# A decoder layer on one core: the first split spread by TensorE, scores on all 128 columns, three groups of heads in one half of a bank

## What is computed

```python
x = _layernorm(x + attn(x))            # latent attention, causal, 256 keys
x = _layernorm(x + xattn(x, ctx_1024)) # 512 context keys + 256 own keys, own ones causal
x = _layernorm(x + ffn(x))             # 64 small MLPs of 16 hidden units each
```

## Time and profile before

| | us |
|---|---|
| median of 3 runs | 291.99 |
| lowest, highest | 291.78, 295.43 |
| the profiled execution | 293.45 |
| its span, first to last instruction | 291.7 |

### The profile page before, as it was taken

The page is one execution under the profiler, slowest core; times in us unless marked ns, Lnnn a source line. Parts: engine busy times, 40 slices in busy tenths (PEclk is TensorE's granted clock), DMA queues, the critical chain, the costliest instruction groups (busy, mean ns, idle before and its releaser), DMA issues.

```text
span 291.7 us, 13772 instructions
## 1 busy us (share of the span) xinstructions
PE 241.0 (83%) x5973; PEld 144.2 (49%) x5973; DVE 194.3 (67%) x429; ACT 159.8 (55%) x367; POOL 99.8 (34%) x250
## 2 busy tenths in 40 slices
PE   8920478689845699999999499999999999999882
PEld 5710336456533446756555156454654465544651
DVE  0830395785232578797999277999889997852652
ACT  1400024455523257676788255988688858879330
POOL 8650074635321142334372101522225212531131
PEclk9985595999977799999999669999999999999998
DMA  4169995101897017353639600000000000000000
GB/s 138 64 202 299 243 205 141 24 8 42 248 186 174 12 57 169 107 117 102 124 106 224 115 3 3 5 5 5 5 3 5 5 5 5 3 5 21 21 18 18
DMA packets 22716, 23.66 MB, mean 81 GB/s; under 512 B 1472, under 2 KB 20224, under 8 KB 22528
## 3 DMA queue, kind: packets, MB, share of 16 engines
q1 hardware_dynamic: 22224, 22.55, 31.7%
q10 hardware_dynamic: 432, 0.23, 0.3%
HBM read 12.62 MB, written 9.96 MB: 77 GB/s over the span
## 4 chain that ended last, share of the span: by engine, by line
PE 42%; DVE 19%; DMA 14%; SPq 9%; issue 7%; ACT 3%; POOL 3%; ACTq 2%; POOLq 0%; DVEq 0%
PE psum L1011 13%; PE psum L1086 10%; DVE pm L869 9%; DMA qk<-shift_rows 6%; DMA qk<-scr_qk 5%; DVE pm L871 4%; PE psum L1106 4%; PE psum L1018 3%; PE psum L958 3%; ACTq L599 2%; ACT probs L774 2%; DMA scr_m<-spl 2%; SPq L635 1%; PE psum L1173 1%; SPq L634 1%
## 5 line engine op out<-in xcount | busy, mean ns | idle before, releaser
L774 ACT ACTIVATE probs<-psum 128x512 f32<-128x512 f32 (+1 forms) x256 | 120.6, 554 | 41.6 <-PE psum L1011 20.9
L1011 PE MATMUL psum<-qk 51*32 51x128 bf16 (+3 forms) x2048 | 63.2, 266 | 31.7 <-DMA qk<-scr_qk 20.9
L871 DVE TENSOR_REDUCE pm<-psum 128x3 f32<-128x384 f32 x128 | 63.5, 550 | 36.6 <-PE psum L1018 36.5
L869 DVE TENSOR_REDUCE pm<-psum 128x1 f32<-128x512 f32 x128 | 79.1, 681 | 7.0 <-PE psum L1011 7.0
L1086 PE MATMUL psum<-probs,v 128*9 128x256 f32 (+1 forms) x1024 | 66.1, 368 | 3.5 <-issue 2.8
L1011 PEld LDWEIGHTS psum<-qk 48*32 48x32 bf16 (+1 forms) x2048 | 35.2, 96 | 56.1 <-DMA qk<-scr_qk 21.5
L1011 PE MATMUL psum<-qk,km 51*32 51x256 bf16 x1024 | 37.9, 278 | 2.8 <-DMA qk<-shift_rows 2.5
L724 POOL TENSOR_SCALAR_AFFINE_SELECT probs<-probs 128x512 f32<-128x512 f32 x32 | 20.3, 640 | 57.0 <-ACT probs L774 56.7
L1086 PEld LDWEIGHTS psum<-probs,v 128*9 128x9 f32 x1024 | 23.2, 91 | 26.0 <-issue 13.8
L1011 PE MATMUL psum<-km,qk 48*32 48x512 bf16 x512 | 35.6, 394 | 0.2
L1018 PE MATMUL psum<-neg,unit_b 64*32 64x256 bf16 x512 | 31.5, 305 | 0.0
(11 more groups left out here) (98 smaller groups left out, 263.7 us busy)
## 6 DMA issues: line engine op xcount, KB each, us to landing
qk<-scr_qk SPq DMA_DIRECT2D x16, 384.0 KB, 6.4
scr_qk<-spl SPq DMA_DIRECT2D x8, 384.0 KB, 5.1
scr_qk<-spl SPq DMA_DIRECT2D x24, 128.0 KB, 5.1
km<-scr_m SPq DMA_DIRECT2D x8, 384.0 KB, 6.8
scr_m<-spl SPq DMA_DIRECT2D x4, 384.0 KB, 3.1
ctxT_sb<-ctxT SPq DMA_DIRECT2D x1, 1024.0 KB, 5.7
scr_m<-spl SPq DMA_DIRECT2D x4, 256.0 KB, 3.5
wb_sb<-wb SPq DMA_DIRECT2D x1, 642.0 KB, 4.5
```

The source lines that it names most:

```text
L774: nc.scalar.activation(probs[:, ring % PRING, r, 0:cols], bank_of(s)[:, 0:cols], ACT.Exp, scale=SCALE).then_inc(exp_done, 1)
L869: nc.vector.tensor_reduce(pm[:, place, 1 + 4 * qt:2 + 4 * qt], m, axis=AX.X, op=ALU.max).then_inc(reduced, 1)
L871: nc.vector.tensor_reduce(pm[:, place, 2:5], own_blocks(m), axis=AX.X, op=ALU.max).then_inc(reduced, 1)
L1011: last = nc.tensor.matmul(o[STRIP * c:STRIP * (c + 1)], lhs[:, STRIP * c:STRIP * (c + 1)], rhs, start=start, stop=stop, skip_group_check=True)
```

## The change

- **First split (unit 0).** No put and take. TensorE lays its parts on their rows: for each of 8 pairs of heads ("rep") six bf16 matmuls against 0/1 matrices `spread`, which GpSimd builds at the start in the place of the context keys of batch 3; ScalarE or VectorE copies the result to `qk`, adding the constant rows by a bias. The scores of a step of unit 0 wait for the two reps of its group.
- **Scores.** `in_tiles` is gone: one matmul on 128 columns takes the place of four on 32. The mask is two matmuls, the second only over half of the block.
- **Heads.** The values lie in zeroed buffers such that the pv of groups 0, 1 and 2 accumulate in one half of bank 7 (up to 27 output rows to a head) and group 3 in the other. ScalarE drains 128 x 512 once to a unit; norm takes 4 matmuls. There are 3 buffers of values for units 4 to 7, blanked by GpSimd after steps 1, 3 and 5; the rows under the context keys come after steps 2, 4, 6 and 8.
- **Start.** 14 warm-up matmuls; the identity and unit matrices are cast by ScalarE; VectorE writes the constant rows for units 1 to 3; the context is loaded right after the weights.
- **Engines.** The low parts of the splits of units 1 to 3 go from GpSimd to VectorE. The last step of a layer norm goes from VectorE to ScalarE, with `-mean * rstd` made by GpSimd (two instructions more).
- **Order.** New costs and `LATE`; `SPL` = 5; a feed-forward's last product waits for the last `wo`.

```diff
-SPL = 3
+SPL = 5
+V2BUFS = 3
...
-BLANK_AFTER = (2, 4, 6)
+VALUES_AFTER = (1, 3, 5)
+BLANK_AFTER = (2, 4, 6, 8)
...
-LATE = [(("qk", 0), 0), (("qk", 1), 0), (("v1", 0), 0), (("qk", 2), 0), (("v1", 1), 0),
-        (("m", 0), 2), (("vm", 0), 4), (("qk", 3), 6), (("m", 1), 8), (("vm", 1), 10), (("m", 2), 16), (("vm", 2), 17),
-        (("m", 3), 20), (("vm", 3), 21)]
+LATE = [(("qk", 0), 0), (("qk", 1), 0), (("qk", 2), 1), (("v1", 0), 0), (("qk", 3), 3), (("v1", 1), 1), (("m", 0), 5),
+        (("vm", 0), 11), (("m", 1), 6), (("vm", 1), 13), (("m", 2), 12), (("vm", 2), 15), (("m", 3), 22),
+        (("vm", 3), 25)]
...
+def replicated(s):
     return s == ("qk", 0)
...
+    return s[0] == "qk" and s[1] < B
...
+        spread = km[:, B - 1, 0:3, :].rearrange("p n (i c) -> p (n i) c", c=P).rearrange("p (i a n) c -> p i a n c", i=2, a=2)
+        v1 = sb("v1", [P, B * QT, VCOLS])
+        v2 = sb("v2", [P, V2BUFS, KT2, VCOLS])
...
+            pool.wait_ge(wa_in, 16)
+            hot = wa_sb[:, WA["hot"]:WA["hot"] + STRIP].rearrange("p (i r d) -> p i r d", i=2, r=2)
+            for a, order in enumerate(MEETING):
+                for slot, part in enumerate(order):
+                    cols = spread[:, :, a, part, :].rearrange("p i (r c) -> p i r c", r=2)
+                    nc.gpsimd.tensor_copy(cols[:, :, :, slot * HS:(slot + 1) * HS], hot).then_inc(spread_ready, 1)
...
-                    if n in BLANK_AFTER:
-                        ones_under_memory(1 + BLANK_AFTER.index(n))
+                    if n in VALUES_AFTER:
+                        blank_values(VALUES_AFTER.index(n))
+                    elif n in BLANK_AFTER:
+                        ones_under_memory(BLANK_AFTER.index(n))
...
+            nc.scalar.activation(ident_b[:, :], ident, ACT.Copy).then_inc(ident_ready, 1)
+            for r in range(2):
+                nc.scalar.activation(half(unit_b, r, HALF)[:, HALF:P], half(ident, r, HALF)[:, HALF * r:HALF * (r + 1)],
+                                     ACT.Copy).then_inc(ident_ready, 1)
             fold_out(4, w1[:, 1, :])
-            fold_out(5, w1[:, 2, :])
...
-                    nc.scalar.activation(headsT[:, t % (2 * NG), :], heads[:, 0:T], ACT.Copy).then_inc(drained, 1)
+                    nc.scalar.activation(headsT[:, t // NG % 2].rearrange("p n t -> p (n t)"), heads, ACT.Copy).then_inc(drained, 1)
...
+                elif what == "apply":
+                    kind_, b = s[1], s[2]
+                    act.wait_ge(rstd_ready, ln_no[s[1:]] + 1)
+                    for i in range(QT):
+                        last = nc.scalar.activation(x1[:, b, i, :], res[:, i, :], ACT.Identity, bias=offset[:, i:i + 1],
+                                                    scale=rstd[:, i:i + 1])
...
-            ones_under(nc.vector, qk[:, 0, :, 1, :]).then_inc(qk_ones[0], 1)
+            for u in range(1, B):
+                ones_under(nc.vector, qk[:, u, :, 1, :]).then_inc(qk_ones, 1)
...
+                    elif what == "rep":
+                        dve.wait_ge(bias_ready, 1)
+                        nc.vector.tensor_copy(qk[:, 0, s[1], 0, :], m[:, 0:T])
+                        nc.vector.tensor_scalar_add(qk[:, 0, s[1], 1, :], m[:, T:], ones_bias[:, 0:1]).then_inc(dve_misc_done, 1)
...
-                    keep_warm(2, bank(n)[:, half_bank * T:(half_bank + 1) * T])
+                    keep_warm(1, bank(n)[:, half_bank * T:(half_bank + 1) * T])
...
+                    elif replicated(("qk", u)):
+                        for a in range(2):
+                            wait_misc(("rep", 2 * group(t) + a))
...
-            def in_tiles(o, lhs, rhs, start, stop):
-                for c in range(HG):
-                    last = nc.tensor.matmul(o[STRIP * c:STRIP * (c + 1)], lhs[:, STRIP * c:STRIP * (c + 1)], rhs, start=start,
-                                            stop=stop, skip_group_check=True)
-                return last
-            def mask(o, r, rows):
-                for c in range(HG):
-                    last = nc.tensor.matmul(o[STRIP * c:STRIP * (c + 1)], half(unit_b, r, HALF), half(rows, r, HALF)[:, c, :, :],
-                                            start=False, stop=True, skip_group_check=True)
+            def mask(o, r, what):
+                rows = half(neg if what == "S" else negT, r, HALF)
+                for n in range(2):
+                    units = half(unit_b, r, HALF)[:, HALF * (1 - n):HALF * (1 - n) + P]
+                    if (what == "S") == (n == 0):
+                        block, part = o, rows
+                    else:
+                        block, part = (o[:, :, HALF:], rows[:, 0:HALF]) if what == "S" else (o[:, :, 0:HALF], rows[:, HALF:])
+                    last = nc.tensor.matmul(block, units, part.unsqueeze(1).to_broadcast([HALF, 2, part.shape[-1]]), start=False,
+                                            stop=(n == 1), skip_group_check=True)
                 return last
...
-                in_tiles(m[:, 0:P], queries[:, 0:P], keys[:, 0:P], True, False)
-                in_tiles(m[:, P:P + T], queries[:, P:T], keys, False, False)
-                return mask(own_blocks(m)[:, 0:3:2, :], r, neg)
+                    return nc.tensor.matmul(m, queries[:, qt * P:(qt + 1) * P], half(km[:, u % B, p, :], r, DATA), start=True,
+                                            stop=True)
+                nc.tensor.matmul(m[:, 0:P], queries[:, 0:P], keys[:, 0:P], start=True, stop=False, skip_group_check=True)
+                nc.tensor.matmul(m[:, P:P + T], queries[:, P:T], keys, start=False, stop=False, skip_group_check=True)
+                return mask(own_blocks(m)[:, 0:3:2, :], r, "S")
...
-                    if k == 0 and t:
-                        pe.wait_ge(drained, t)
+                    if k == 0 and g == 0 and t:
+                        pe.wait_ge(drained, t // NG)
...
+                        at = VJ * j + VG * g
+                        end, at = at + HS + 1, at - (HS + 1) * (g if g < NG - 1 else 0)
+                        if k == 0 and g == 0:
+                            end = at + VG
+                        o = heads[STRIP * j:STRIP * j + end - at, (T if g == NG - 1 else 0):][:, q0:T]
...
-                        last = nc.tensor.matmul(heads[STRIP * j:STRIP * j + HS + 1, q0:T], v, weights, start=(k == 0),
-                                                stop=(k == len(key_tiles(t)) - 1))
+                        last = nc.tensor.matmul(o, v[:, at:end], weights, start=(k == 0 and g in (0, NG - 1)),
+                                                stop=(k == len(key_tiles(t)) - 1 and g >= NG - 2), skip_group_check=True)
...
                         for qt in range(QT):
-                            for g in range(NG):
-                                at, cols = ORDER.index((u, g)) % (2 * NG), HG * (HS + 1)
-                                n = qt * NG + g
-                                last = nc.tensor.matmul(m[:, n * cols:(n + 1) * cols], headsT[:, at, qt * P:(qt + 1) * P],
-                                                        used_rows, start=True, stop=True)
+                            for n, cols in ((0, (NG - 1) * HG * (HS + 1)), (1, HG * (HS + 1))):
+                                o = m[:, qt * NH * (HS + 1) + n * (NG - 1) * HG * (HS + 1):][:, 0:cols]
+                                last = nc.tensor.matmul(o, headsT[:, at % 2, n, qt * P:(qt + 1) * P], used_rows[n], start=True,
+                                                        stop=True)
...
+                        parts = spl[:, split_no[("qk", 0)] % SPL, :, :]
+                        for a in range(2):
+                            for n in range(PARTS):
+                                last = nc.tensor.matmul(m[:, a * T:(a + 1) * T], strip(spread[:, i, a, n, :], j, STRIP),
+                                                        strip(parts[:, 5 - 2 * n if a else 2 * n, :], j, STRIP),
+                                                        start=(a == 0 and n == 0), stop=(n == PARTS - 1), skip_group_check=True)
```

296 lines of the change are left out of this document (177 added, 119 removed).

## The result

| | before | after |
|---|---|---|
| median us | 291.88 (4 runs) | 278.77 (4 runs) |
| lowest, highest | 288.89, 295.43 | 275.87, 281.61 |
| the profiled execution, its span | 293.45, 291.7 | 280.01, 278.3 |

The ratio is 0.955, with a 95% interval from 0.940 to 0.970: faster by 4.5%, some 13 us. Some executions of every kernel here run a few per cent longer at a lower clock; the medians include them and the ratios don't, so that the two can differ.

The account below looks back on a forecast made before the run. Waits were taken to bound units 0 to 3 and VectorE's maxima units 4 to 7. Start 14 + units 0 to 3 56 + units 4 to 7 139.5 + mask 1 + tail 36 = 246.5, less 0.3: 246 us, range 231 to 270.

Parts of the forecast that it names:

- 26 + 30 = 56: Units 0 to 3: from first score to unit 4's start, a chain of 64 us unchanged, shortened to 56.
- 139.5: Units 4 to 7: 151.5 us less 7 for the applies and 5 for half of the hole.
- 1 for the mask: TensorE: the wide mask adds 5.6 us of columns over the run, 1 us of it on the path.
- Forecast 14: Start: the first score comes at 14 us, not 33.3, or 16.9 us earlier with slow casts.
- no gap of over 3 us: Sign that the forecast is right: no gap of over 3 us between units 2 and 3.
- Half of the hole: Units 4 to 7: half the wait for small DMAs at 158 to 168 us goes, 5 us of 10.
- 7 us: Units 4 to 7: 22 of 24 layer-norm applies leave VectorE for ScalarE, gaining 7 us.
- 6.93 us to a step, all VectorE: Units 4 to 7: context maxima at 6.93 us a step bind on VectorE, 111 us for 16 steps.
- So I take nothing: TensorE: merging scores, 3,072 matmuls fewer, gains nothing since columns bind; upper bound 29 us.
- slower rival: Wide matmul loads do not hide within a half of TensorE: 316 us, chance 0.05.
- 0, with ends of 3 either way: Tail: moving work of the last two layer norms to GpSimd and ScalarE costs 0, ends of 3 us.
- Rival 1: Only the start gains; waits for reloads and small DMAs move instead of going: 259.5 or 272 us, chance 0.22.

Follow-up runs that it names:

- e5: Changed kernel with the first split sent through scratch like all others, without the spread by TensorE: 289.67 us, ratio 0.985 to the kernel before.
- e15: Changed kernel with the loads of x and the biases (640 KB) issued behind the take of unit 3: 276.52 us, ratio 0.956 to the kernel before.
- e1: Changed kernel with the list `LATE` taken back to that of the kernel before: 287.02 us, ratio 0.990 to the kernel before.
- e14: Changed kernel with one planner cost, s_ahead, at 2300 in place of 2200, same work in another order: 293.96 us, ratio 1.014 to the kernel before.
- e2: Changed kernel with the layer norm's apply back on VectorE, without GpSimd's two small instructions: 275.93 us, ratio 0.951 to the kernel before.
- e13: Changed kernel with maxima over context keys taken over 256 of 512 columns (work left out): 279.35 us, beside 291.92 for the kernel before.
- e4: Changed kernel with every score and mask matmul cut into four narrow ones: 313.62 us, ratio 1.082 to the kernel before.
- e6: Kernel before with only its score matmuls made wide, masks still narrow: 367.66 us, beside 293.1 for the kernel before.
- e10: Changed kernel with only its mask matmuls cut into narrow pieces: 355.0 us, ratio 1.223 to the kernel before.
- e16: Changed kernel with apply back on VectorE, bulk puts and takes held behind small DMAs on SyncE, x loaded late: 264.38 us, ratio 0.914 to the kernel before.
- e9: Kernel before, in its own order, with scores and masks all wide in the changed kernel's form: 282.76 us, ratio 0.969 to the kernel before.
- e3: Changed kernel with the small DMAs of maxima of units 4 to 7 issued by ScalarE, not SyncE: 286.66 us, ratio 0.988 to the kernel before.
- e8: Changed kernel without the mask matmuls in the scores of the own keys (work left out): 285.62 us, beside 293.1 for the kernel before.

## Why the prediction was wrong

Two terms carry 25 of the 32 us over the forecast: "26 + 30 = 56" for units 0 to 3, measured 68.1, and "139.5" for units 4 to 7, with 1 for the mask, measured 153.2.

- **The start.** Forecast 14, measured 16.20. TensorE's eight reps come in one row ahead of the scores in its order, and ScalarE made all their copies, where I had two reps ahead and two engines. Within the own range of 14 to 20. The mechanism was right; the spread itself is 9 of the 17 us (e5).
- **Units 0 to 3.** The failed term is "26 + 30 = 56". From the first score to the norm of unit 0 it was 34.3 us, as before (33.9), and from there 33.8. I had shortened the chain for drains, norms and reloads and had let nothing lengthen it but 8 us of GpSimd. What lengthened it were bytes: from the first score to the norm of unit 0 the share of the DMA engines is 0.72, where it was 0.48. e15 moved 640 KB of them and won 3.9 us by step 16. The rest of it is order: e1 and e14 move step 16 by 12 and 13 us without changing the work. Unit 3's gap of 19.7 us from step 11 to 12 went only in part: 9.7 us stay (60.06 to 69.77), against the sign "no gap of over 3 us". The late reload in it went, as forecast (the longest wait of TensorE for a DMA there is 0.8 us); what stays is filled with products of other stages. Nor was it `LATE`: e1, with the old list, has 58.38 to 66.27 there.
- **Units 4 to 7.** Forecast 139.5 + 1, measured 153.2. "Half of the hole", 5 us: it stayed, 8.0 us, three steps earlier in the run. "7 us" for the applies: nothing (e2). "6.93 us to a step, all VectorE": VectorE's load can go without the step getting shorter (e13), and two steps of 6.93 us are not the mean, which from step 22 to 31 was 8.4 us in before and is 8.8 in after. Rows of a chain that runs through one engine say which engine was last, not that it is alone.
- **TensorE.** "So I take nothing" for the merging was wrong by some 8 us in the old order and by up to 34 in the new one, and here the forecast had luck: with narrow pieces the changed kernel is slower than before (e4), so that even the sign hung on a term put at nothing. The step that failed is the choice between two prices, columns and issue. Both were beside the point, as narrow or wide pieces made under 2 us in the steady part; what counted was the length of the code where DMA engines are busy, which no term of mine had. The rows were there: gaps of "issue" of 5.8 us in before.
- **Wide loads.** The slower rival is refuted for one width: the steady part is no longer with wide pieces than with narrow ones. Where widths are mixed inside a bank, something else costs 70 to 75 us (e6, e10), and the change had turned every score and mask at once.
- **The tail.** "0, with ends of 3 either way" for the layer norms: 5 us worse in the profile, and e2 shows that it is the move of the apply (36.5 us with it back on VectorE, 41.9 without).
- **The rivals.** Rival 1 described it best, waits that move and don't go; it gave 259.5 to 272. It had the chain (78 against 84.3) and the hole right, and lacked the apply's nothing and the tail.

In parts measured alone: the merging some 8 to 34 us, the spread 10, against the apply at -4; the order at anything from 0 to 14. They don't add up to one sum, since each part changes where the transfers meet the small DMAs.

## What to carry to other kernels

Where DMA engines are busy, ask of each transfer which small DMA will be issued within its flight, and move the bulk, not the queue: this gave some 11 us here with no work changed (275.93 in e2, 264.38 in e16). Count instructions as traffic: an engine's code comes over the same DMA engines. Don't change the width of matmuls every two to four of them inside a bank: turn scores and masks together or not at all. And test an order's neighbours (one cost by a few per cent) before a gain is put down to a change.

## What I had not expected of the hardware

- Code: TensorE's gaps of up to 5.1 us that have no releaser, with 0.87 MB of instructions in 313 us, nearly all beside bulk transfers, each ending 1.2 to 1.7 us behind a packet of code (e4).
- A cast of 128 x 128 on VectorE took 2.82 us beside GpSimd's writing of constant rows, and 0.15 us with GpSimd idle (before, e9).
- Groups of matmuls of 128 and of 32 columns in one bank hardly overlap: a group of four narrow ones starts 0.53 us behind two wide ones, and the clock stays at 0.50 for 27 us with TensorE busy throughout (e6).
- A pair of DMAs of 3 KB took 11.6 us from its issue on ScalarE's queue to the first matmul, beside bulk transfers on SyncE's (e3).
- Without its mask matmuls the kernel ran at a lower mean clock, 0.85 in place of 0.92, and longer (e8).
